# Slot loop of a hypergraph layer: gates and coefficients found a round ahead, three of eight tiles scaled on ScalarE

## The reference

```python
h = x @ W
agg = einsum('ben,bnf->bef', softmax(masked s), h)         # one row per hyperedge
beta = sigmoid((h @ a_gn)[:, None, :] + (agg @ a_ge)[:, :, None])
all_he = elu(beta * h + (1 - beta) * agg)                  # per node and hyperedge
coefs1 = softmax(where(H > 0, se[:, None, :], NEG), -1)    # se: score of elu(agg)
g = einsum('bne,benf->bnf', coefs1, all_he)
out = mix of g and a neighbour mean (adj / deg)
```

## Time and profile before

| | us |
|---|---|
| three runs | 2384.14 median (2382.97 to 2387.27) |
| profiled execution | 2385.27, its span 2383.1 |
| mean granted TensorE clock | 0.928 of full |
| busy over the span: TensorE, VectorE, ScalarE, GpSimd | 2077.2, 2068.9, 1395.7, 918.3 |
| slot loop in the trace | some 170 to 362 |

### The profile page before, as it was taken

How to read it: one execution, slowest core, us unless ns; L and a number is a source line. 1 busy time by engine, 2 the same in 40 slices (tenths; PEclk the granted TensorE clock), 3 DMA queues, 4 the chain that set the end, 5 groups by cost and what they waited for, 6 DMA issues and landing times. The chain is left out here.

```text
span 2383.1 us, 61686 instructions
## 1 busy us (share of the span) xinstructions
PE 2077.2 (87%) x26510; PEld 1370.8 (58%) x26510; DVE 2068.9 (87%) x2791; ACT 1395.7 (59%) x2215; POOL 918.3 (39%) x526
## 2 busy tenths in 40 slices
PE   3858887647878779999999999999999999998886
PEld 2644545434547556666666666666666666665654
DVE  7558873658965669999999999999999999999995
ACT  2422221248963156776776766666666766776784
POOL 0029990013640024444444444444444444442221
PEclk8869998867888879999999999999999999999997
DMA  3000000043420132111121121021211210122432
GB/s 122 1 1 0 0 0 1 2 79 63 75 37 2 22 78 51 38 42 42 38 51 28 35 49 42 29 55 38 51 34 37 51 42 29 33 55 51 76 68 46
DMA packets 172949, 94.76 MB, mean 40 GB/s; under 512 B 158520, under 2 KB 159736, under 8 KB 172304
## 3 DMA queue, kind: packets, MB, share of 16 engines
q1 hardware_dynamic: 172688, 90.94, 17.2%
HBM read 80.09 MB, written 10.83 MB: 38 GB/s over the span
## 5 line engine op out<-in xcount | busy, mean ns | idle before, releaser
L603 ACT ACTIVATE x_sb<-x_sb,hid_neg_max 128x1024 f32<-128x1024 f32 x576 | 661.7, 1154 | 288.8 <-DVE hid_neg_max L518 288.5
L527 DVE STREAM_TRANSPOSE hid_weights_t<-x_sb 128x1024 f32<-128x1024 f32 x576 | 709.5, 1232 | 1.6 <-ACT x_sb L603 1.2
L518 DVE CUSTOM_DVE_ANT_0 x_sb<-ps_score,adj_mask,row_scale 128x1024 f32<-128x1024 f32 x512 | 636.4, 1243 | 16.9 <-PE ps_score L386 15.8
L406 PE MATMUL ps_low<-hid_weights_t,hid_x_rep 32*64 32x256 f32 x18432 | 576.2, 383 | 10.2 <-ACT hid_share L633 9.7
L386 PE MATMUL ps_score<-hid_y_hi,hid_xs 128*128 128x512 f32 x1152 | 524.1, 455 | 32.8 <-DVE hid_neg_max L518 27.2
L406 PEld LDWEIGHTS ps_low<-hid_weights_t,hid_x_rep 32*64 32x64 f32 x18432 | 392.4, 132 | 168.3 <-issue 96.6
L386 PE MATMUL ps_score<-hid_y_lo,hid_xs 128*128 128x512 f32 x1152 | 459.0, 398 | 0.0
L713 POOL TENSOR_TENSOR hid_z<-hid_z,hid_inv_cols 128x1024 f32<-128x1024 f32 x64 | 194.3, 3035 | 552.2 <-ACT hid_z L611 552.2
L386 PEld LDWEIGHTS ps_score<-hid_y_hi,hid_xs 128*128 128x128 f32 x1152 | 218.4, 190 | 259.9 <-issue 153.6
L386 PEld LDWEIGHTS ps_score<-hid_y_lo,hid_xs 128*128 128x128 f32 x1152 | 219.7, 191 | 44.4 <-issue 15.1
L705 POOL TENSOR_TENSOR hid_y_wide<-hid_y_wide,hid_y_hi 128x1024 f32<-128x1024 f32 x64 | 153.7, 2402 | 194.5 <-ACT hid_y_wide L594 194.5
(11 more groups left out here) (330 smaller groups left out, 3132.8 us busy)
## 6 DMA issues: line engine op xcount, KB each, us to landing
hid_inv_cols<-hid_inv_rows SPq DMA_DIRECT2D x64, 512.0 KB, 3.7
hid_x_rep<-hid_row_space SPq DMA_DIRECT2D x64, 256.0 KB, 5.8
gat_x_rep<-gat_row_space SPq DMA_DIRECT2D x32, 256.0 KB, 5.4
adj_rows<-in_adj SPq DMA_DIRECT2D x8, 512.0 KB
gat_e_wide<-gat_e_space SPq DMA_DIRECT2D x8, 512.0 KB, 6.4
marks<-hid_mark_rows SPq DMA_DIRECT2D x8, 512.0 KB, 4.8
x_sb<-in_x SPq DMA_DIRECT2D x2, 1024.0 KB, 6.3
gat_row_space<-gat_wh SPq DMA_DIRECT2D x8, 256.0 KB, 4.3
```

The costliest lines, as they stand in the source:

```text
L406: ins = pe.matmul(m.ps_low[c * F:(c + 1) * F, a, 0:NT * Q], x_rep[a * Q:(a + 1) * Q, batch_of(g) % 2, b, :], weights_t[a * Q:(a + 1) * Q, ...
L518: dve.tensor_tensor_reduce(ring[:, i % RING, :], m.ps_score[:, i % 2, :], mask, scale, HUGE, ALU.add, ALU.min, neg_max[:, g % 2, t:t + 1]) ...
L527: dve.transpose(weights_t[:, g % 2, :, t, :], ring[:, i % RING, :].rearrange("p (b j) -> p b j", j=Q)).then_inc(tile_turned, 1)
L603: act.activation(ring[:, i % RING, :], ring[:, i % RING, :], ACT.Exp, scale=-1.0, bias=neg_max[:, g % 2, t:t + 1], accum_out=row_sum[:, g ...
```

## The change

It moves the next round's tests into the round, changes how the edge rank is compared, and moves three of GpSimd's eight multiplies a round to ScalarE.

- `rank` is no longer counted down. A [128, 1] number `level` is counted up and `rank == level` is compared, twice: once into `next_pick` behind the first two differences, once into `pick` behind difference(7).
- TensorE makes the next round's small products from `next_pick` behind `add_diff(2)`; ahead of the loop stands one set for round 0.
- VectorE asks for the next gate and coefficients behind share(3) and difference(5) (`ask`, `ask_coef`), and finishes them behind share(5) and difference(7) (`settle_coef`), together with the comparison for `pick` and the step of `level`.
- ScalarE makes the two small exps behind the exp of tile 4. For tiles 1, 4 and 7 it scales the share with eight activations of 64 columns, one for each batch, with `pool_coef` as the scale; GpSimd then only adds.

```diff
 @block.tensor
-                with pe.Fori(0, slot_count(pe)) as k:
-                    pe.wait_ge(picked, k + 1)
+                def find_small(picked_cols):
                     for t in range(NT):
-                        ins = pe.matmul(..., pick[:, t * P:(t + 1) * P],
+                        ins = pe.matmul(..., picked_cols[:, t * P:(t + 1) * P],
                                         picks[:, B * F:], start=True, stop=True)
                     ins.then_inc(small_ready, 1)
 
+                pe.wait_ge(picked, 1)
+                find_small(pick)
+                with pe.Fori(0, slot_count(pe)) as k:
...
                     for t in range(NT):
                         add_diff(t)
+                        if t == 2:
+                            pe.wait_ge(next_picked, k + 1)
+                            pe.wait_ge(coef_ready, k + 1)
+                            find_small(next_pick)
                         if 1 <= t and t + 2 < NT:
                             row_pair(t + 2)
 @block.scalar
-                    act.wait_ge(beta_asked, k + 1)
-                    act.activation(beta[:], beta[:], ACT.Exp, scale=-1.0).then_inc(beta_exped, 1)
-                    act.wait_ge(coef_asked, k + 1)
-                    act.activation(coef[:], coef[:], ACT.Exp).then_inc(coef_exped, 1)
+                    def scale_share(t):
+                        if t == ACT_TILES[0]:
+                            act.wait_ge(coef_taken, k + 1)
+                        act.wait_ge(share_ready, k * NT + t + 1)
+                        s = by_batch(share[:, t % 4, :])
+                        for b in range(B):
+                            ins = act.activation(s[:, b, :], s[:, b, :], ACT.Copy, scale=pool_coef[:, t, b:b + 1])
+                        ins.then_inc(act_scaled, 1)
+
                     for t in range(NT):
                         act.wait_ge(blend_ready, k * NT + t + 1)
                         act.activation(blend_exp[:, t % 2, :], row_banks(t)[0], ACT.Exp,
                                        bias=minus_one[:, 0:1]).then_inc(blend_exped, 1)
+                        if t - 1 in ACT_TILES:
+                            scale_share(t - 1)
+                        if t == 4:
+                            act.wait_ge(beta_asked, k + 2)
+                            act.activation(next_beta[:], next_beta[:], ACT.Exp, scale=-1.0).then_inc(beta_exped, 1)
+                            act.wait_ge(coef_asked, k + 2)
+                            act.activation(coef[:], coef[:], ACT.Exp).then_inc(coef_exped, 1)
+                    scale_share(NT - 1)
 @block.gpsimd
                     for t in range(NT):
-                        pool.wait_ge(share_ready, k * NT + t + 1)
                         s = share[:, t % 4, :]
-                        pool.tensor_tensor(by_batch(s), by_batch(s), along(pool_coef, t), ALU.mult)\
-                            .then_inc(scaled, 1)
-                        pool.wait_ge(scaled, k * NT + t + 1)
+                        if t in ACT_TILES:
+                            pool.wait_ge(act_scaled, k * len(ACT_TILES) + ACT_TILES.index(t) + 1)
+                        else:
+                            pool.wait_ge(share_ready, k * NT + t + 1)
+                            pool.tensor_tensor(by_batch(s), by_batch(s), along(pool_coef, t), ALU.mult)\
+                                .then_inc(scaled, 1)
+                            pool.wait_ge(scaled, ...)
                         pool.tensor_tensor(rows[:, t, :], rows[:, t, :], s, ALU.add)\
                             .then_inc(share_added, 1)
 @block.vector
+                def ask(small_count):
+                    dve.wait_ge(small_ready, small_count)
+                    dve.tensor_tensor(next_beta[:], small[:, :, B:2 * B], gate[:], ALU.add).then_inc(beta_asked, 1)
...
                     scale_away(0)
                     scale_away(1)
-                    dve.wait_ge(coef_exped, k + 1)
-                    link(dve.tensor_tensor(coef[:], coef[:], small[:, :, 16:17].to_broadcast([P, NT, B]),
-                                           ALU.mult))
-                    dve.nop().then_inc(coef_ready, 1)
-                    link(dve.tensor_tensor(coef_sum[:], coef_sum[:], coef[:], ALU.add))
-                    link(dve.tensor_scalar(rank[:], rank[:], -1.0, None, ALU.add))
+                    dve.tensor_scalar(next_pick[:], rank[:], level[:, 0:1], None, ALU.is_equal)\
+                       .then_inc(next_picked, 1)
                     for t in range(NT):
                         add_share(t)
                         if t + 2 < NT:
                             scale_away(t + 2)
-                        if t + 3 == NT:
+                        if t == 3:
+                            ask(k + 2)
+                            dve.wait_ge(coef_taken, k + 1)
+                            ask_coef(link)
+                        if t == 5:
+                            dve.wait_ge(beta_exped, k + 2)
+                            link(dve.tensor_scalar(next_beta[:], next_beta[:], 1.0, None, ALU.add))
+                            link(dve.reciprocal(beta[:], next_beta[:]))
                             dve.wait_ge(rows_ready, k * NT + NT)
-                            dve.tensor_scalar(pick[:], rank[:], 0.0, None, ALU.is_equal)\
+                            dve.tensor_scalar(pick[:], rank[:], level[:, 0:1], None, ALU.is_equal)\
                                .then_inc(picked, 1)
-                    dve.wait_ge(picked, k + 2)
+                            dve.wait_ge(picked, k + 2)
+                            dve.wait_ge(coef_exped, k + 2)
+                            settle_coef(link)
+                            link(dve.tensor_scalar(level[:], level[:], 1.0, None, ALU.add))
```

More of the change, by code:

```diff
@@ L2034, in hypergraph_layer @@
                 sem("share_ready"), sem("share_added"))
+            act_scaled, next_picked = sem("act_scaled"), sem("next_picked")
+            level = psb("level", [P, 1])
+            next_pick = psb("next_pick", [P, N], F32R)
+            next_beta = psb("next_beta", [P, NT, B])
+            ACT_TILES = (1, 4, 7)
             small = m.ps_misc[:, 0, 0:NT * 18].rearrange("p (t c) -> p t c", t=NT)
@@ L2117, in _, with ask_coef @@
             def _(dve):
-                dve.memset(minus_one[:], -1.0).then_inc(step, 1)
-                dve.memset(coef_sum[:], 0.0).then_inc(step, 1)
-                dve.wait_ge(step, 2)
-                dve.nop().then_inc(rows_taken, 3)
-                dve.nop().then_inc(coef_taken, 1)
-                steps = 6
-                dve.tensor_scalar(pick[:], rank[:], 0.0, None, ALU.is_equal).then_inc(picked, 1)
-                dve.wait_ge(picked, 1)
-                with dve.Fori(0, slot_count(dve)) as k:
-                    link = Chain(dve, step, 2 + k * steps)
-                    dve.wait_ge(small_ready, k + 1)
-                    dve.tensor_tensor(beta[:], small[:, :, B:2 * B], gate[:], ALU.add).then_inc(beta_asked, 1)
-                    dve.wait_ge(coef_taken, k + 1)
+                def ask(small_count):
+                    dve.wait_ge(small_ready, small_count)
+                    dve.tensor_tensor(next_beta[:], small[:, :, B:2 * B], gate[:], ALU.add).then_inc(beta_asked, 1)
+                def ask_coef(link):
                     link(dve.tensor_tensor(coef[:], small[:, :, 0:B], best[:], ALU.subtract))
@@ L2135, in _, with settle_coef @@
                                              op0=ALU.min, op1=ALU.mult).then_inc(coef_asked, 1)
-                    dve.wait_ge(beta_exped, k + 1)
-                    link(dve.tensor_scalar(beta[:], beta[:], 1.0, None, ALU.add))
-                    link(dve.reciprocal(beta[:], beta[:]))
+                def settle_coef(link):
+                    link(dve.tensor_tensor(coef[:], coef[:], small[:, :, 16:17].to_broadcast([P, NT, B]),
+                                           ALU.mult))
+                    dve.nop().then_inc(coef_ready, 1)
+                    link(dve.tensor_tensor(coef_sum[:], coef_sum[:], coef[:], ALU.add))
+                first = Chain(dve, step)
+                first(dve.memset(minus_one[:], -1.0))
+                first(dve.memset(coef_sum[:], 0.0))
+                first(dve.memset(level[:], 0.0))
+                dve.nop().then_inc(rows_taken, 3)
+                dve.tensor_scalar(pick[:], rank[:], level[:, 0:1], None, ALU.is_equal).then_inc(picked, 1)
+                dve.wait_ge(picked, 1)
+                first(dve.tensor_scalar(level[:], level[:], 1.0, None, ALU.add))
+                ask(1)
+                ask_coef(first)
+                dve.wait_ge(beta_exped, 1)
+                first(dve.tensor_scalar(next_beta[:], next_beta[:], 1.0, None, ALU.add))
+                first(dve.reciprocal(beta[:], next_beta[:]))
+                dve.wait_ge(coef_exped, 1)
+                settle_coef(first)
+                steps = 6
+                with dve.Fori(0, slot_count(dve)) as k:
+                    link = Chain(dve, step, first.n + k * steps)
```

10 lines of the change are left out of this document (8 added, 2 removed).

## The result

The changed kernel took 2416.8 us (2414.33 to 2418.77, four runs), the kernel before beside it 2385.56 (four runs): the ratio is 1.0131 with a 95% interval of 1.0114 to 1.0149. Its profiled execution took 2418.77 us, 33.5 more than the 2385.27 of before; its span is 2416.8 (before 2383.1). The forecast was 2411.

The account below looks back on a forecast made before the run. VectorE's chain was taken to bound the round. Tile part +4.2 and turn -0.88 make +3.3 a round; eight gaps 26.4, last tile part 4.2 and tail -3.5 sum to +27.1, giving 2411 us, range 2394 to 2422.

Parts of the forecast that it names:

- VectorE's chain sets the round: Whole round of the slot loop, 20.60 us: VectorE's chain sets it, and GpSimd, with four share buffers, just keeps up.
- The turn gains 0.88 with the low clock: From share(7)'s end to the next share(0): 7.25 us becomes 6.37 with TensorE's clock dropped, 4.80 at full clock.
- Tests +0.95: Tile part: eight small TensorE matmuls behind the addition of tile 2 delay exp(3) and share(3) by 0.95 us a round.
- Asking +0.85: Tile part: VectorE's three operations asking for gate and coefficients, behind share(3) and difference(5), add 0.85 us a round.
- Block +2.4: VectorE's add 1, reciprocal, comparison, settling, sum and level step behind difference(7), ahead of share(6), add 2.4 us a round.
- Scalings cost 0 at 0.20 us a piece: ScalarE's eight activations for each of three tiles take 1.6 us a tile and fit beside other work, costing 0.
- Tail -3.5: After the last share(7): GpSimd has no backlog and ends 3.1 us behind it instead of 6.60, gaining 3.5 us once.
- head 0 to 2: Loop entry: the loop's count is read behind the first tests instead of beside them, 0 to 2 us once, taken as 0.
- The full clock at the turn: Rival: TensorE's clock stays up at the turn; a round costs +1.75 us, 2399 in all; chance 0.22.
- With hardly any load on GpSimd: Ports-free rival: VectorE's waits for GpSimd go; tile part +2.4 us, a round costs nothing at full clock, 2383; chance 0.10.

Follow-up runs that it names:

- the 16 extra matmuls: Changed kernel plus 16 matmuls of 512 columns behind a round's last addition, into a PSUM bank nobody reads: 2402.18 us, ratio to before 1.0066.
- the version without extra matmuls: Kernel before with level compare, gate, coefficient and sum scratch in PSUM, and ScalarE scaling tiles 1 and 4 in halves: 2375.06 us, ratio 0.9956.
- 8 extra matmuls: Kernel before with level, PSUM scratch, ScalarE scaling tiles 1 and 4 in halves, and eight 256-column matmuls behind the last addition: 2364.56 us, ratio 0.9908.

## Why the prediction was right

- *VectorE's chain sets the round.* Right: taking 1.5 us out of that chain alone gave the round 0.84 back, with GpSimd's work unchanged; then the piece of the chain up to the first difference set the turn.
- *The turn gains 0.88 with the low clock.* It gained 0.74. The granted clock over the turn was 0.59 to 0.76 at all eight, so the drop came at every one. That the clock is the difference between 4.8 and 6.5 us is shown by the 16 extra matmuls. That the size came out so near is partly luck: I had one value, 6.37, from one turn of before, and the eight run from 6.05 to 7.62.
- *Tests +0.95.* +0.90; right, and TensorE is where they cost: share(2) to share(3) is 2.68 us with and without ScalarE's scalings.
- *Asking +0.85.* It took 1.31 us (237.76 to 239.07) and made share(4) 1.07 later; share(5) got 0.21 back. Right. ("At most 0.25 us" of idle time ahead of a share was misread: before share(2) the kernel before has 0.35. Ahead of share(4), where it counts, it has 0.16.)
- *Block +2.4.* The step that was mis-sized: +2.90. The rows gave 3.75 us for the block and it took 4.00: settling and sum 1.20 in place of 0.62 (the sum waits 0.57 for GpSimd, which I had put into the range only), the comparison 0.91 in place of 1.10, the rest 1.89 in place of 2.03. I then took 0.25 off "since GpSimd is busy less", and that reason is wrong. With all eight multiplies on GpSimd the add of 1 took 0.58 us; with five it took 1.08. In a tile part that repeats to 0.01 us the wait is what is left of GpSimd's instruction at that moment, the same in every round, and no share of busy time gives it. 0.5 us in nine rounds is 4.5 of the 6.4 us that the sum was short; the turn is 1.1 of them, the head 0.8, the tail 0.3, and the tests gave 0.4 back.
- *Scalings cost 0 at 0.20 us a piece.* The size was wrong: 2.01 us for eight. My row was of activations that read PSUM. The Trainium skill, "ScalarE: Activation LUTs", section "What ACT_TABLE_LOAD costs", gave 0.24 and the trace agrees: (2.01 - 0.34) / 7 = 0.24. (0.34 us is what one of them takes, read where a row shows one by itself, in the version without extra matmuls.) "The row decides" was the wrong call between the two: the row was of another form. As a delay of exp(3) it cost nothing, because the tests had delayed exp(3) by as much; without them it did, 0.69 us at share(3), in the run with ScalarE's part alone. But the scalings had a cost that I had put at nothing: by moving GpSimd's instructions they made the tile part 0.82 us longer (17.99 against 17.17) and the turn 0.30 shorter, so that a round is 0.51 longer (24.50 against 23.99) and the loop 4.4 (229.79 against 225.44 from the first comparison to GpSimd's last add); the medians are 1.8 apart.
- *Tail -3.5, head 0 to 2.* -3.2 and +0.8. The head isn't shown to be the moved reading of the count: it is 11.41 us in the run with GpSimd's work left out, which has the new order, and 12.64 in the run with ScalarE's part alone, which has the old one.
- *Rivals.* The full clock at the turn, forced by extra matmuls, gives 2402 where I had 2399. With hardly any load on GpSimd the tile part grew by 2.3 us where the rival said 2.4, and a round at the full clock took 20.4 us against 20.6 before, as the rival said; but the clock still fell at four turns, and the kernel came to 2389, so even then it isn't faster than before.

## What to carry to other kernels

Work that is taken out of a stretch where every engine waits for VectorE and put into one where VectorE is busy gains nothing, however early its result is there; look first for the engine's idle time and put it there (2.5 us a round in the one place and 0.5 in the other for the same five operations). VectorE and GpSimd on SBUF can wait for each other's instruction in progress. So lay a small operation beside GpSimd's timeline and count what is left of the instruction there, in every round of a steady loop (0.13 to 0.88 us here), not a share of busy time; or keep its scratch in PSUM. Less work on GpSimd can make such waits longer. When a chain is shortened, ask what TensorE's clock does in the new gap.

## What the runs showed of the hardware

- A VectorE operation of 64 columns with two SBUF inputs, or with a constant from SBUF to SBUF, took 0.2 us alone and, beside GpSimd, up to 1.1, by what was in progress there (the add of 1: 0.40, 0.58, 0.63 and 1.08 in four kernels); with its scratch in PSUM, so that at most one input lay in SBUF, 0.22 to 0.23 beside GpSimd too. The Trainium skill, "SBUF — State Buffer", section "Who interferes with whom", states both conditions.
- A comparison of 1024 columns against a value per partition takes 0.74 us without a wait, the count-down by a constant 0.69.
- Eight activations of 64 columns, SBUF to SBUF with a scale from SBUF, take 2.01 us; such ones from PSUM start 0.20 us apart.
- Clock: it fell at all eight turns of the changed kernel, ahead of which TensorE idled 4.46 us; at six of the kernel before (idle 0.53) and at one of that kernel with the level alone (idle 0.54); at five of eight in the version without extra matmuls (idle 0.92), though each round is the same; at none with 16 or 8 extra matmuls. The length of the gap alone doesn't decide it.
